# Looped weight streaming in a spectral product, and column-tiled transform matmuls

## The reference

```python
x = x + conv3x3(gn(x))             # 3 x 3 convolution with bias
x = x + scan(gn(x))                # gated recurrence over the 64 image columns
x = x + spectral_low(gn(x))        # rfft2, 16 x 16 modes mixed over channels, irfft2
x = x + spectral_full(gn(x))       # rfftn, all modes mixed over channels, irfftn, bias
```

## Time and profile before

| | us |
|---|---|
| median of three runs | 592.81 |
| lowest and highest | 592.74 and 593.74 |
| the profiled execution | 593.76 |
| its span, first to last instruction | 592.0 |
| TensorE busy | 535.6 (90%) |
| VectorE, ScalarE, GpSimd busy | 474.7, 392.5, 300.8 |
| mean granted TensorE clock, share of 2.4 GHz | 0.993 |

### The profile page before, as it was taken

How to read it: one execution, slowest core, us unless ns; L and a number is a source line. 1 busy time by engine, 2 the same in 40 slices (tenths; PEclk the granted TensorE clock), 3 DMA queues, 4 the chain that set the end, 5 groups by cost and what they waited for, 6 DMA issues and landing times.

```text
span 592.0 us, 26552 instructions
## 1 busy us (share of the span) xinstructions
PE 535.6 (90%) x10404; PEld 428.3 (72%) x10404; DVE 474.7 (80%) x1270; ACT 392.5 (66%) x832; POOL 300.8 (51%) x424
## 2 busy tenths in 40 slices
PE   3999999599999999999999999988788887999996
PEld 2333333487777777777778999988488776999995
DVE  7778977479899998989898777888877796477876
ACT  3555889767777777777677966775478875556441
POOL 7765654156666666666665212035577799121000
PEclk9999999989999999999999999999999999999999
DMA  6900000011111111111112200001337876003324
GB/s 227 385 7 0 2 2 4 14 39 44 36 44 37 42 41 39 44 36 44 40 40 63 100 2 0 0 1 48 98 114 245 252 227 207 5 1 143 142 123 162
DMA packets 21297, 45.90 MB, mean 78 GB/s; under 512 B 5104, under 2 KB 15600, under 8 KB 20352
## 3 DMA queue, kind: packets, MB, share of 16 engines
q1 hardware_dynamic: 20160, 44.97, 24.2%
q10 hardware_dynamic: 672, 0.15, 0.1%
q0 software_dynamic: 416, 0.07, 0.1%
HBM read 28.53 MB, written 8.39 MB: 62 GB/s over the span
## 4 chain that ended last, share of the span: by engine, by line
PE 43%; DVE 33%; issue 11%; ACT 5%; POOL 3%; DVEq 2%; DMA 1%; SPq 0%; POOLq 0%; ACTq 0%
DVE spec L1333 8%; PE psum L662 8%; PE psum L835 8%; DVE spec L1325 6%; DVE spec L1336 5%; PE psum L777 5%; PE psum L913 5%; PE psum L793 5%; PE psum L929 5%; DVE small L1218 4%; PE psum L902 3%; PE psum L761 2%; POOL work L373 2%; ACT work L299 2%; DVE spec L1328 2%
## 5 line engine op out<-in xcount | busy, mean ns | idle before, releaser
L697 PE MATMUL psum<-spec,matrices 128*32 128x128 f32 x3024 | 110.0, 279 | 14.1 <-ACT spec L1020 7.3
L697 PEld LDWEIGHTS psum<-spec,matrices 128*32 128x32 f32 x3024 | 76.9, 110 | 46.0 <-ACT spec L1020 46.0
L704 PE MATMUL psum<-spec,matrices 128*32 128x128 f32 x3024 | 108.1, 276 | 1.3 <-DMA spec<-work 1.3
L551 POOL TENSOR_TENSOR spec<-spec 64x128 f32<-64x128 f32 x126 | 70.7, 561 | 72.9 <-DVE spec L1336 72.9
L704 PEld LDWEIGHTS psum<-spec,matrices 128*32 128x32 f32 x3024 | 86.1, 111 | 4.2 <-issue 3.9
L662 PE MATMUL psum<-spec,matrices 128*64 128x512 f32 x384 | 85.6, 603 | 1.0 <-ACT spec L954 1.0
L835 PE MATMUL psum<-work 128*32 128x128 f32 x2368 | 70.9, 274 | 14.9 <-issue 9.4
L835 PEld LDWEIGHTS psum<-work 128*32 128x32 f32 x2368 | 64.3, 110 | 21.3 <-issue 20.2
L529 POOL TENSOR_SCALAR spec<-image,small 32x960 f32<-32x960 f32 (+1 forms) x48 | 55.5, 1157 | 33.6 <-PE psum L662 19.7
L545 POOL TENSOR_TENSOR image<-image,spec 128x128 f32 (+1 forms) x128 | 69.4, 542 | 0.0
L373 ACT ACTIVATE work<-work 32x768 f32<-32x768 f32 x66 | 55.7, 843 | 15.7 <-PE psum L835 11.1
(11 more groups left out here) (154 smaller groups left out, 927.1 us busy)
## 6 DMA issues: line engine op xcount, KB each, us to landing
work<-w_dram SPq DMA_DIRECT2D x33, 512.0 KB, 4.4
spec<-work SPq DMA_DIRECT2D x124, 64.0 KB, 1.9
image<-x_dram SPq DMA_DIRECT2D x3, 2048.0 KB, 11.7
out_dram<-image SPq DMA_DIRECT2D x3, 2048.0 KB, 6.3
image<-x_dram SPq DMA_DIRECT2D x4, 512.0 KB, 5.7
work<-w_dram SPq DMA_DIRECT2D x1, 2048.0 KB, 7.7
out_dram<-image SPq DMA_DIRECT2D x4, 512.0 KB, 2.9
kept<-const_dram SPq DMA_DIRECT2D x1, 192.0 KB, 5.4
```

The costliest lines, as they stand in the source:

```text
L551: nc.gpsimd.tensor_tensor(straddled(h, ROWS_01, 0), *of, ALU.subtract).then_inc(lower_ready[h], 1)
L697: last = mm(psum[QUARTERS[hm], 4 * h + g, 0:HB], sv[:, g, QUARTERS[hm]], moving[hm], start=starts, stop=True)
L704: last = mm(psum[q, 4 * h + g, 0:HB], sv[:, 3 + g, q], e, start=True, stop=stops)
```

## The change

1. **Loop.** TensorE runs steps 0 to 5 of the large product written out and the other 27 as a loop of nine passes over three steps. The waits in the loop compare with values that are computed from the loop's counter.
2. **Weights.** Three buffers of two halves each (256 KB) take the place of four of 512 KB. A half has its own semaphore. The first half of step s is loaded when the first half of step s - 3 has been used (new semaphore `half_mixed`), the second when step s - 3 is done. TensorE waits for the second half in the middle of the step. SyncE issues two DMAs for a step, steps 0 to 5 written out and the rest in a loop of nine.
3. **Banks.** From step 5 on the results go round three PSUM banks (`bank_of`), and step s waits for s - 3 copies rather than s - 4.
4. **Transforms.** Each 128 x 128 product of `over_w`, `over_h` and of both backward products is issued as two products of 64 stationary columns, each writing half of the PSUM partitions (`in_two`). The moving operands and the results are the same; so are the transposes.

```diff
-        w3_m = [w2_m[:, 1024 * i:1024 + 1024 * i] for i in range(4)]
+        w3_m = [[w2_m[:, 1024 * i + 512 * h:1024 * i + 512 * h + 512] for h in range(2)] for i in range(3)]
...
+        def bank_of(s_):
+            return s_ if s_ < 5 else (s_ + 1) % 3
...
+            def weights_of(s_, chunk_=None):
+                for h in range(2):
+                    if isinstance(s_, int) and s_ < 3:
+                        if h == 0:
+                            sp.wait_ge(l2_done, s_ + 1)
+                    else:
+                        sp.wait_ge((half_mixed, mix_done)[h], s_ - 2)
+                    src = w9[:, 512 * h:512 * h + 512] if chunk_ is None else w3[:, ds(chunk_ * 1024 + 512 * h, 512)]
+                    yield src, h
+            for s_ in range(6):
+                for src, h in weights_of(s_, None if s_ == 4 else chunk_of(s_)):
+                    sp.dma_start(w3_m[s_ % 3][h], src).then_inc(w3_in[s_ % 3][h], 16)
+            with sp.Fori(0, (STEPS - 6) // 3) as i:
+                for k in range(3):
+                    for src, h in weights_of(i * 3 + (k + 6), i * 3 + (k + 5)):
+                        sp.dma_start(w3_m[k][h], src).then_inc(w3_in[k][h], 16)
...
+            def in_two(out, stationary, moving):
+                for o in (slice(0, P // 2), slice(P // 2, P)):
+                    last = mm(out[o], stationary[:, o], moving, start=True, stop=True)
+                return last
...
-                        last = mm(psum[:, (c // 3 + 4) % 8, 4 * PADK * (c % 3):4 * PADK * (c % 3) + 4 * PADK],
-                                  bw[:, :, c // 2, c % 2], cm["fw"],
-                                  start=True, stop=True)
+                        last = in_two(psum[:, (c // 3 + 4) % 8, 4 * PADK * (c % 3):4 * PADK * (c % 3) + 4 * PADK],
+                                      bw[:, :, c // 2, c % 2], cm["fw"])
...
                 for k in range(CHUNK_T // 4):
+                    if k == 2 and second is not None:
+                        pe.wait_ge(*second)
...
+                    if k == 1 and second is not None:
+                        last.then_inc(half_mixed, 1)
...
-            for s_ in range(STEPS):
+            for s_ in range(6):
                 if s_ == 4:
                     pe.wait_ge(stat3, STAT3)
                 mix(s_)
+            with pe.Fori(0, (STEPS - 6) // 3) as i:
+                for k in range(3):
+                    mix(i * 3 + (k + 6), k, i)
...
-                        last = mm(psum[:, n, P * i:P * i + P], kh[:, :, 2 * n + i // 2, i % 2], cm["ih"],
-                                  start=True, stop=True)
+                        last = in_two(psum[:, n, P * i:P * i + P], kh[:, :, 2 * n + i // 2, i % 2], cm["ih"])
...
-                v.tensor_copy(chunk(chunk_of(s_)), psum[:, chunk_of(s_) % 4, :]).then_inc(y_moved, 1)
+                v.tensor_copy(chunk(chunk_of(s_)), psum[:, bank_of(s_), :]).then_inc(y_moved, 1)
```

More of the change, by code:

```diff
@@ L203, in program @@
         w2_in = sem("w2_in")
-        w3_in = [sem(f"w3_in{i}") for i in range(4)]
+        w3_in = [[sem(f"w3_in{i}{h}") for h in range(2)] for i in range(3)]
         conv_zeroed, scan_zeroed, pads_zeroed, eps_set = map(sem, ("conv_zeroed", "scan_zeroed", "pads_zeroed", "eps_set"))
@@ L249, in program @@
         scaled_ready, spread_act, spread_pool = sem("scaled_ready"), sem("spread_act"), sem("spread_pool")
-        mix_done, y_moved = sem("mix_done"), sem("y_moved")
+        half_mixed, mix_done, y_moved = sem("half_mixed"), sem("mix_done"), sem("y_moved")
         nyq_moved, sym, sym_pool = sem("nyq_moved"), sem("sym"), sem("sym_pool")
@@ L792, in over_h @@
                     for b in range(GB):
-                        last = mm(psum[:, n, 2 * H * b:2 * H * b + 2 * H], bh[:, b, n % 2, 4 * (n // 2):4 * (n // 2) + 4], cm["fh"],
-                                  start=True, stop=True)
+                        k4, e = 4 * (n // 2), n % 2
+                        for i, half in enumerate((slice(k4, k4 + 2), slice(k4 + 2, k4 + 4))):
+                            last = mm(psum[P // 2 * i:P // 2 * (i + 1), n, 2 * H * b:2 * H * b + 2 * H], bh[:, b, e, half],
+                                      cm["fh"], start=True, stop=True)
                     last.then_inc(h_done, 1)
@@ L819, in _, with tiles @@
             over_h(NG - 1, True)
-            def tiles(weights, planes, bank, done, starts=True):
-                wt = weights.rearrange("p (t r o) -> p t r o", r=2, o=C)
+            def tiles(weights, planes, bank, done, starts=True, second=None):
+                wt = [w_.rearrange("p (t r o) -> p t r o", r=2, o=C) for w_ in weights]
                 pl = planes.rearrange("p (t m) -> p t m", m=PLANES)
                 for k in range(CHUNK_T // 4):
+                    if k == 2 and second is not None:
+                        pe.wait_ge(*second)
                     for r, from_, to in ((0, 64, 192), (1, 0, 128)):
@@ L834, in tiles @@
                             t = 4 * k + q
-                            last = mm(o, wt[:, t, r, :], pl[:, t, from_:to], start=starts and k == 0 and r == 0,
-                                      stop=r == 1, skip_group_check=True)
+                            last = mm(o, wt[t // 8][:, t % 8, r, :], pl[:, t, from_:to],
+                                      start=starts and k == 0 and r == 0, stop=r == 1, skip_group_check=True)
+                    if k == 1 and second is not None:
+                        last.then_inc(half_mixed, 1)
                 last.then_inc(done, 1)
@@ L851, in _ @@
                 pe.wait_ge(l2_neg, 3 * (c + 1))
-                tiles(w2_m[:, 1024 * c:1024 * c + 1024], diag[c % 2], c, l2_done)
+                tiles([w2_m[:, 512 * h:512 * h + 512] for h in (2 * c, 2 * c + 1)], diag[c % 2], c, l2_done)
             for s_ in range(4):
@@ L861, in _, with mix @@
             keep_warm(WARM_NORM, cm["ident"])
[L864 to L872, removed]
-            for s_ in range(STEPS):
+            def mix(s_, k=None, i=None):
+                first = isinstance(s_, int) and s_ < 6
+                slot = s_ % 3 if first else k
+                use = s_ // 3 * 16 + 16 if first else i * 16 + 48
+                pe.wait_ge(w3_in[slot][0], use)
+                pe.wait_ge(spread_act, s_ * 2 + 2)
+                pe.wait_ge(spread_pool, s_ * 2 + 2)
+                if not first or s_ == 5:
+                    pe.wait_ge(y_moved, s_ - 3)
+                tiles(w3_m[slot], diag[slot], bank_of(s_) if first else (k + 1) % 3, mix_done, not first or s_ >= 4,
+                      (w3_in[slot][1], use))
+            for s_ in range(6):
                 if s_ == 4:
@@ L928, in back @@
                             at_ = 256 * i + 128 * x_
-                            last = mm(psum[:, n, at_:at_ + 128], kwv[:, x_, n, i], cm["iw"], start=True, stop=True)
+                            last = in_two(psum[:, n, at_:at_ + 128], kwv[:, x_, n, i], cm["iw"])
                     last.then_inc(c_done, 1)
```

## The result

The changed kernel takes 584.9 us (median, 584.2 to 585.9) against 593.2 for the kernel before (592.7 to 593.7): ratio 0.9862, 95% interval 0.9845 to 0.9879. The forecast was 583.2, with a range of 579.5 to 590.0. The profiled execution took 584.2 and has a span of 582.4, 9.6 less than the one before.

What follows compares the result with a forecast made beforehand. TensorE was taken to bound the transforms; in the large product its code gaps, then ScalarE in steps 9 to 16 and GpSimd from step 20. Transforms -5.4 and large product -4.25 give -9.65: 592.81 to 583.2 us, range 579.5 to 590.

Steps and rivals of the forecast that it cites:

- The pace of 109 ns: Transforms: paired column tiles stream 128 columns in 109 ns, against 117.8 on the full array; 0.56 us a stage and group.
- The change of shape, put at 0.09: Transforms: each change of tile shape on TensorE costs 0.09 us; fifteen added, 1.2 us counted against the gain.
- -5.4: Transforms: total from issuing products as pairs, -6.6 us of faster streaming plus 1.2 us of shape changes.
- -4.25: Large product: total from the loop, -3.2 us before GpSimd's step 20 and -1.05 us of TensorE's lag at the end.
- The rival that a jump fetches its code again: Large product: eight loop jumps each stall for code, 0.41 to 4.30 us apiece; 603 us at 2.5 each; chance 0.05.
- 32.65 us: Large product from step 20: GpSimd works without a wait and is the bound, so this stretch stays unchanged.
- In steps 9 to 16 it is ScalarE: Large product: two copies and a Nyquist move, 2.14 us a step, bound these steps, so gaps there cost next to nothing.
- The sign that I had named: Large product: ScalarE still taking 2.14 us a step in steps 9 to 16 would show the forecast right.
- the 3.2 that I took: Large product: GpSimd starts step 20 3.2 us earlier, at 469.7 to 470.4 instead of 473.15.
- The end of -5.9: Large product: the most favourable total, -5.9 us, if the early gaps of 0.97 and 0.59 fall away too.
- the 1.76 us: Large product: TensorE's pace per step, used to give a half load 4.4 us between issue and use.
- 0.41 as the other end: Large product: computed waits and jump cost nothing behind queued matmuls; if exposed, 8 x 0.41 = 3.3 us.

Runs made afterwards that it cites:

- the pairs alone: The kernel before with only the transforms' products issued as pairs of 64-column tiles; 588.5 us, against 593.2 to 593.9 before.
- the loop alone: The changed kernel with the four transform products on the full array again, keeping loop, half loads and three banks; 590.3 us.
- with quarters: The changed kernel with the transforms' products on quarters of 32 columns instead of pairs of 64; 591.5 us.
- a body of 4.6 packets: The changed kernel with TensorE's loop as three passes over nine steps, 1152 instructions, instead of nine passes over three; 585.8 us.

## Why the prediction was right, point by point

**Pairs.** The pace of 109 ns, set between the quarters' 110 and the convolution's 107.5, is 109.6. The change of shape, put at 0.09 from one row that gives 0.20 - 0.118 = 0.08, is 0.075 to 0.095. The stages add up to -5.2 us against -5.4, both in the kernel after and with the pairs alone. The rule of the Trainium skill on loads of tiles that share their rows ("TensorE: Matmul & The Clock Gate", Part 3) would have made the round longer; the runs with pairs and with quarters do not agree with it for column tiles.

**Loop.** -4.25 was forecast; the trace has -4.5, the run with the loop alone -3.1 by its median and -3.7 in its large product. The mechanism is shown from both sides: written out again, the gaps return with everything else kept. The rival that a jump fetches its code again is refuted by 4 packets against 16 over the stage, and by a body of 4.6 packets that stays. So the rule in the Trainium skill ("Runtime: NRT & Kernel Launch", Instruction fetch mechanics) that a jump beyond two pages stalls for a fetch is not what these runs show on TensorE.

**GpSimd from step 20.** 32.65 us were kept in the sum, 32.63 came; the lag behind it was put at 2.15, it is 2.2.

**The step that failed.** "In steps 9 to 16 it is ScalarE" was wrong: without the Nyquist moves these steps gain 0.6 us, not 2.5. The trace before could not tell the two apart by rate, since TensorE with its gaps took 2.15 us a step and ScalarE 2.14. It could by order: TensorE starts step 17 at 469.81 (the start of a single matmul), 1.6 us after ScalarE's copies for it ended at 468.21, and the chain holds matmuls and issue there. So the gaps of these steps did count. The sign that I had named, ScalarE still at 2.14 us a step, came (455.51 to 457.64 in the kernel after), but an engine can keep that pace without being the bound.

That the sum was hardly hurt is luck. GpSimd's step 20 was put 35.7 to 36.4 us into the stage and came at 35.7, 3.5 us earlier than before against the 3.2 that I took. But 0.7 of that was gained ahead of the last early gap, where I counted on nothing: two gaps, 0.60 and 0.64, came in place of three, 0.97, 0.52 and 0.59, and the matmul after the last one starts 16.04 us into the stage rather than 16.77. Why one gap is gone is not shown. Behind it 2.8 us were gained, where I counted on 3.2. (The end of -5.9 adds up to -5.8, and it left out the gap of 0.52.)

A loop step also costs more than the 1.76 us, the pace of written-out code, that I gave TensorE. In the starts of single matmuls two steps of three take 1.75 to 1.77 us and the one with the jump 1.91 to 1.95, so a step takes 1.82 and the jump costs TensorE nearly 0.2 us each time. I had costed it at nothing, behind queued matmuls, with 0.41 as the other end.

**The median** came 1.7 us above the forecast although the profiled execution fits it to 0.1: it is the fastest of its four, while the one before was the slowest of its four. The difference between medians, 8.3, is the better measure of the gain, and the forecast of 9.65 was 1.3 too large by it.

## What to carry to other kernels

On an engine whose instructions are shorter than the time in which their code arrives, look for issue gaps at a fixed count of instructions: a loop removes them, and it needs no small body. A float32 matmul on the full array can be faster as two on half the columns if nothing else has to change shape often. After either, look for the engine that never waits in the stage, and move work from it to one that does. Where the profile names the engine that ended a wait, compare with the time at which that engine had finished: here it named ScalarE where GpSimd was the last. And a rate over a few steps is no bound while the buffers let that engine run ahead.

## What the runs showed of the hardware

- Written-out TensorE code of 27.5 ns per load and matmul pauses 0.3 to 1.4 us after nearly every 252 instructions; packets are 16 KB, and two steps with their gap take 4.3 us.
- Code of 1152 instructions and its waits stays on TensorE between passes of a loop; a jump back shows as nearly 0.2 us when 14 ns instructions are queued.
- In float32 the full array takes 117.8 ns for 128 moving columns, two tiles of 64 take 109.6 together and four of 32 about the same (14.13 and 14.26 us for two stages).
- A change of tile shape costs TensorE 0.075 to 0.095 us.
